# Group norm in token order with crossbar transposes of x, and a new order of the work

## The reference, cut to what matters

```python
def _gn(v, G=32, eps=1e-5):
    g = v.reshape(B_, H_, W_, G, C_ // G)
    m = jnp.mean(g, axis=(1, 2, 4), keepdims=True)
    s = jnp.var(g, axis=(1, 2, 4), keepdims=True)
    return ((g - m) / jnp.sqrt(s + eps)).reshape(v.shape)

qkv = x @ qkv_w.T + qkv_b            # q += x @ la_q.T @ lb_q.T, v += x @ la_v.T @ lb_v.T
attn = einsum('bqd,bkd->bqk', q * scale, k)      # 12 heads of 64, 196 x 196 per image and head
attn = attn + rel_h[..., None] + rel_w[..., None, :]   # q against tables of relative positions
out = softmax(attn) @ v
x + out @ proj_w.T + proj_b          # x was normalized by _gn before the attention only
```

## Time and profile before

| | |
|---|---|
| median of 3 runs | 3372.39 us (3372.22 to 3372.78) |
| the profiled execution | 3373.03 us, its span 3371.3 us |
| TensorE busy, share of the span | 3297.2 us, 98% |
| VectorE busy | 2528.2 us, 75% |
| ScalarE busy | 2098.2 us, 62% |
| SyncE's DMA queue, share of 16 engines | 49.8% |
| granted TensorE clock, mean | 0.991 |

### The profile page before, as it was taken

The page is one execution under the profiler, slowest core; times in us unless marked ns, Lnnn a source line. Parts: engine busy times, 40 slices in busy tenths (PEclk is TensorE's granted clock), DMA queues, the critical chain, the costliest instruction groups (busy, mean ns, idle before and its releaser), DMA issues.

```text
span 3371.3 us, 80148 instructions
## 1 busy us (share of the span) xinstructions
PE 3297.2 (98%) x31984; PEld 2130.7 (63%) x31984; DVE 2528.2 (75%) x5970; ACT 2098.2 (62%) x5651; POOL 35.8 (1%) x65
## 2 busy tenths in 40 slices
PE   7689999999999999999999999999999999999998
PEld 4456666666666666666666666666666666666665
DVE  7577777777777777777777777777777777777764
ACT  2466666666666666666666666666666666666664
POOL 0000000000000000000000000000000000000000
PEclk9799999999999999999999999999999999999999
DMA  3145664555555556565555555555565555565554
GB/s 128 42 96 109 120 122 103 115 113 112 118 121 107 113 112 114 116 121 107 110 116 113 112 123 118 101 117 111 110 127 120 100 118 108 111 126 122 103 106 105
DMA packets 1091412, 376.13 MB, mean 112 GB/s; under 512 B 916696, under 2 KB 1071320, under 8 KB 1091040
## 3 DMA queue, kind: packets, MB, share of 16 engines
q1 hardware_dynamic: 1075206, 333.63, 49.8%
q10 hardware_dynamic: 15834, 37.37, 3.9%
HBM read 86.60 MB, written 38.54 MB: 37 GB/s over the span
## 4 chain that ended last, share of the span: by engine, by line
PE 94%; DVE 2%; ACT 1%; issue 0%; DMA 0%; POOL 0%; SPq 0%; POOLq 0%; DVEq 0%
PE ring L556 51%; PE ring L623 17%; PE score L599 9%; PE o_ps L613 7%; PE ring L578 3%; PE ring L637 3%; PE ring L629 3%; ACT prob L682 1%; PE ring L642 0%; PE ring L563 0%; DVE split L789 0%; DVE row_max L769 0%; DVE rel_sb L762 0%; DVE split L781 0%; DVE rel_sb L756 0%
## 5 line engine op out<-in xcount | busy, mean ns | idle before, releaser
L556 PE MATMUL ring<-xn_hi,w_hi 128*128 128x392 f16 x3456 | 1143.2, 331 | 4.8 <-DVE xn_lo L839 4.6
L556 PE MATMUL ring<-xn_lo,w_hi 128*128 128x392 f16 x3456 | 1139.8, 330 | 0.0
L556 PE MATMUL ring<-xn_hi,w_lo 128*128 128x392 f16 x3456 | 1139.3, 330 | 0.5 <-issue 0.5
L682 ACT ACTIVATE prob<-score,neg_max,exp_scale 98x196 f32<-98x196 f32 x1536 | 769.8, 511 | 252.9 <-DVE neg_max L773 245.4
L769 DVE TENSOR_REDUCE row_max<-score 98x4 f32<-98x784 f32 x384 | 373.3, 972 | 273.2 <-PE score L599 272.1
L789 DVE SCALAR_TENSOR_TENSOR split<-prob,row_inv,split 98x196 f16<-98x196 f32 x1536 | 545.0, 417 | 7.8
L556 PEld LDWEIGHTS ring<-xn_hi,w_hi 128*128 128x128 f16 x3456 | 342.3, 99 | 260.7 <-issue 7.7
L556 PEld LDWEIGHTS ring<-xn_hi,w_lo 128*128 128x128 f16 x3456 | 338.8, 98 | 237.9 <-issue 3.6
L556 PEld LDWEIGHTS ring<-xn_lo,w_hi 128*128 128x128 f16 x3456 | 338.9, 98 | 208.3 <-issue 1.9
L623 PE MATMUL ring<-o_hi,w_hi 128*128 128x392 f16 x1152 | 380.2, 330 | 1.4 <-DVE o_lo L798 1.4
L623 PE MATMUL ring<-o_lo,w_hi 128*128 128x392 f16 x1152 | 379.8, 330 | 0.0
(11 more groups left out here) (118 smaller groups left out, 4896.7 us busy)
## 6 DMA issues: line engine op xcount, KB each, us to landing
y_sb<-in_x SPq DMA_DIRECT2D x192, 196.0 KB
out<-y_sb SPq DMA_DIRECT2D x192, 196.0 KB
x_sb<-in_x ACTq DMA_DIRECT2D x31, 1176.0 KB
rel_q<-rel_sb SPq DMA_DIRECT2D x128, 122.5 KB, 2.4
stage<-in_L_conv_qkv_w SPq DMA_DIRECT2D x3, 2304.0 KB, 15.4
turned<-split SPq DMA_TRANSPOSE x384, 4.2
rel_q<-rel_sb SPq DMA_DIRECT2D x128, 24.5 KB, 1.9
v_tok<-v_split SPq DMA_TRANSPOSE x192, 3.4
```

Of the source, the lines that this page charges most:

```text
L556: last = T.matmul(ring[:, bank, 0:NT], w[:, c, 128 * j:128 * j + 128], xx[:, par, c, :], start=(c == 0 and part == 0), stop=(c == CT - 1 a ...
L682: last = A.activation(prob[:, head, half, :], score[0:HALF, head, TOK * half:TOK * half + TOK], ACT.Exp, bias=neg_max[:, k % 2, i:i + 1], ...
```

## The change

The group norm is made on x as it is loaded, 98 tokens on partitions, instead of on transposed x, and the crossbar DMA does the turning afterwards, on fp16 parts.

- X and M are gone from TensorE, ScalarE and VectorE, and with them `xT`, `bn_stats` and `bn_aggr`.
- A (two a pair): VectorE sums x over the 24 channels of each group and two tiles, `tensor_reduce` of 98 x 1536. G0: a matmul with `gmean`, now 98 x 98 and filled with 1/(24 x 196), sums over tokens and spreads the means to all 98 partitions. B (two): subtract the mean, in place in `x_sb`. U (two): ScalarE squares into `squares`, which lies in the memory of `xs`. D (two): VectorE sums the squares. G1: variances of the 64 groups on partitions; `pow` on GpSimd; E makes a diagonal matrix; G2 spreads it by a matmul with ones. H (two): multiply, in place. I (two): ScalarE makes the fp16 high part in `xs`; L (two): VectorE the low part. XT (four): crossbar DMA of 112 x 1536 fp16 each, from `xs` to `xn`.
- Q, K and V read `xn[:, par, part, :, c, 0:98]`, four runs of 98 columns. Q0 waits once, for all four XT. The weights are no longer taken with a stride in `prepare`.
- LD waits until L of the pair before is done (`x_sb` is now in use until then) and stands in slot 5 instead of 6; A0 of the same pair stands at the end of VectorE's slot 6.
- `y_sb` has two buffers instead of three, `yT` one instead of two: ScalarE's Y now waits until Z of the block before is done.
- The five order lists are new. K and V stand a slot or so earlier in places, R1 has moved to slot 10 on VectorE and ScalarE. In SyncE's list CB, T0 and VT0 of a round stand ahead of the stores ST 4 and 5 and of the reloads.
- The memories that are zeroed have semaphores of their own, waited for at the first use.

The diff, cut to its core:

```diff
-YS = 3
+YS = 2
 PE_ORDER = (
+    each("S", 0, 0) + each("P", 1, 10) + each("Z", 2, 5) + each("V", 0, 0) + each("K", 0, 1)
+    + each("S", 0, 1) + each("P", 1, 11) + each("G", -1, 1) + each("V", 0, 1) + each("G", -1, 2) + each("Y", 1, 0)
+    + each("S", 0, 2) + each("P", 0, 0) + each("K", 0, 2) + each("Y", 1, 1) + each("Z", 1, 0)
+    + each("S", 0, 3) + each("P", 0, 1) + each("Y", 1, 2) + each("Z", 1, 1) + each("V", 0, 2)
+    + each("S", 0, 4) + each("P", 0, 2) + each("Z", 1, 2) + each("K", 0, 3) + each("Q", -1, 0)
...
+    + each("S", 0, 8) + each("P", 0, 6) + each("G", -2, 0) + each("Q", -1, 4, 5)
+    + each("S", 0, 9) + each("P", 0, 7) + each("K", 0, 5) + each("R", -1, 0) + each("Y", 1, 3) + each("R", -1, 1)
     + each("S", 0, 10) + each("P", 0, 8) + each("R", -1, 2, 3, 4) + each("V", 0, 5) + each("Y", 1, 4) + each("Z", 1, 3)
+    + each("S", 0, 11) + each("P", 0, 9) + each("K", -1, 0) + each("Y", 1, 5) + each("Z", 1, 4))
 ACT_ORDER = (
+    each("Y", 2, 5) + each("U", -1, 1) + soft(0) + each("V", 0, 0)
...
+    + each("Y", 1, 0) + each("I", -1, 0) + each("N", 0, 2) + each("K", 0, 2) + each("T", 0, 2) + each("I", -1, 1)
...
+    + each("Q", -1, 0) + each("P", 0, 3) + soft(5) + each("V", 0, 3) + each("LD", -2, 0)
...
+    + each("R", -1, 1, 2) + each("N", 0, 10) + each("R", -1, 3, 4) + each("T", 0, 10) + each("V", 0, 5)
+    + each("Y", 1, 4) + each("U", -2, 0) + each("P", 0, 9) + each("N", 0, 11) + each("K", -1, 0) + each("T", 0, 11))
 DVE_ORDER = (
+    each("S", 0, 0) + each("D", -1, 1) + soft(0) + each("Z", 2, 4) + each("V", 0, 0) + each("Z", 2, 5)
+    + each("S", 0, 1) + each("G", -1, 1) + each("K", 0, 1) + each("P", 1, 11) + each("E", -1, 0) + soft(1)
+    + each("G", -1, 2) + each("V", 0, 1) + each("H", -1, 0)
+    + each("S", 0, 2) + each("H", -1, 1) + each("N", 0, 2) + each("K", 0, 2) + each("T", 0, 2) + each("L", -1, 0)
+    + each("S", 0, 3) + each("Z", 1, 0) + each("P", 0, 1) + each("L", -1, 1) + soft(3)
...
+    + each("S", 0, 6) + each("Q", -1, 1) + each("N", 0, 6) + each("K", 0, 4) + each("T", 0, 6) + each("A", -2, 0)
+    + each("S", 0, 7) + each("Q", -1, 2) + each("P", 0, 5) + soft(7) + each("V", 0, 4) + each("A", -2, 1)
+    + each("S", 0, 8) + each("Q", -1, 3) + each("G", -2, 0) + soft(8) + each("Q", -1, 4) + each("B", -2, 0)
+    + each("S", 0, 9) + each("Q", -1, 5) + each("P", 0, 7) + each("N", 0, 9) + each("K", 0, 5) + each("T", 0, 9)
+    + each("R", -1, 0)
+    + each("S", 0, 10) + each("R", -1, 1, 2) + each("N", 0, 10) + each("R", -1, 3, 4) + each("T", 0, 10) + each("V", 0, 5)
     + each("S", 0, 11) + each("Z", 1, 3) + each("P", 0, 9) + each("N", 0, 11) + each("K", -1, 0) + each("T", 0, 11)
+    + each("B", -2, 1) + each("D", -2, 0))
 SP_ORDER = (
+    each("CB", 0, 0) + each("T", 0, 0) + each("VT", 0, 0)
+    + each("ST", 2, 4, 5) + each("T", 0, 1) + each("VT", 0, 1)
+    + each("LY", 1, 0) + each("XT", -1, 0) + each("LY", 1, 1) + each("T", 0, 2)
+    + each("XT", -1, 1, 2) + each("ST", 1, 0) + each("XT", -1, 3) + each("T", 0, 3) + each("LY", 1, 2)
+    + each("VT", 0, 2) + each("ST", 1, 1) + each("T", 0, 4) + each("LY", 1, 3)
+    + each("ST", 1, 2) + each("T", 0, 5) + each("VT", 0, 3) + each("LY", 1, 4)
...
+    + each("VT", 0, 5) + each("ST", 1, 3) + each("T", 0, 11) + each("LY", 1, 5))
...
+                elif kind == "XT":
+                    part, image = k // 2, k % 2
+                    wait(sp, xs_lo_made if part else xs_hi_made, 2 * p + image + 1)
+                    sp.sem_inc(sp_go, 1)
+                    sp.dma_start_transpose(xn[:, p % 2, part, 2 * image:2 * image + 2].rearrange("p b c r -> p (b c) r"),
+                                           xs[0:ROWS, part, 2 * image:2 * image + 2].rearrange("r b c -> r (b c)")
+                                           ).then_inc(xn_in, 16)
...
-                        if kind == "Q" and k == 0 and c % 2 == 0:
-                            wait(pe, xn_lo_made, 3 * p + c // 2 + 1)
+                        if kind == "Q" and k == 0 and c == 0:
+                            wait(pe, xn_in, 64 * p + 64)
...
+                    wait(act, done["Z"], 6 * p + k)
...
+                elif kind == "A":
+                    if k == 0:
+                        wait(dve, x_in, 16 * p + 16)
+                    two = slice(2 * k, 2 * k + 2)
+                    V.tensor_reduce(sums[:, k, :], x_sb[:, two, :].rearrange("p b (g c) -> p g b c", c=GP),
+                                    AX.XY, ALU.add).then_inc(summed, 1)
...
+                elif kind in ("B", "H"):
+                    wait(dve, read["G"], 3 * p + (1 if kind == "B" else 3))
+                    by_group = x_sb[:, 2 * k:2 * k + 2, :].rearrange("p b (g c) -> p b g c", c=GP)
+                    of = (mean if kind == "B" else rstd)[:, k:k + 1, :]
+                    V.tensor_tensor(by_group, by_group, of.unsqueeze(3).broadcast_to([HALF, 2, GROUPS, GP]),
+                                    ALU.subtract if kind == "B" else ALU.mult
+                                    ).then_inc(centred if kind == "B" else normed, 1)
```

More of the change, by code:

```diff
@@ L577, in _ @@
                                             "p (g i w) -> p g i w", i=n_rows, w=W)[:, :, i, :]
-                                    last = T.matmul(cols, tab[rows, ax, row, 32 * head:32 * head + 32], mov,
+                                    last = T.matmul(cols, tab[rows, ax, row, :], mov,
                                                     start=(part == 0), stop=(part == 2))
@@ L687, in _ @@
                     wait(act, row_inv_made, 12 * p + k + 1)
+                    if p == 0 and k == 0:
+                        act.wait_ge(split_zeroed, 1)
                     wait(act, pv_done, 12 * p + k - 1)
@@ new lines, in _ @@
+                elif kind == "A":
+                    if k == 0:
+                        wait(dve, x_in, 16 * p + 16)
+                    two = slice(2 * k, 2 * k + 2)
+                    V.tensor_reduce(sums[:, k, :], x_sb[:, two, :].rearrange("p b (g c) -> p g b c", c=GP),
+                                    AX.XY, ALU.add).then_inc(summed, 1)
+                elif kind == "D":
+                    wait(dve, squared, 2 * p + k + 1)
+                    two = slice(2 * k, 2 * k + 2)
+                    V.tensor_reduce(sums[:, k, :], squares[:, two].rearrange("p b (g c) -> p g b c", c=GP),
+                                    AX.XY, ALU.add).then_inc(summed, 1)
+                elif kind == "G" and k == 1:
+                    wait(dve, done["G"], 3 * p + 2)
+                    V.tensor_scalar(var_eps[:, :], ring[0:2 * GROUPS, bank, 0:1], EPS, None,
+                                    ALU.add).then_inc(read["G"], 1)
+                elif kind == "E":
+                    wait(dve, inv_dev_made, p + 1)
+                    V.tensor_scalar(diagonal[:, :], ident[0:2 * GROUPS, 0:2 * GROUPS], inv_dev[:, :], None,
+                                    ALU.mult).then_inc(diagonal_made, 1)
+                elif kind == "G":
+                    wait(dve, done["G"], 3 * p + k + 1)
+                    to = mean if k == 0 else rstd
+                    V.tensor_copy(to[:, :, :].rearrange("p n g -> p (n g)"),
+                                  ring[0:HALF, bank, 0:2 * GROUPS]).then_inc(read["G"], 1)
+                elif kind in ("B", "H"):
[5 more added lines that the diff above has]
+                                    ).then_inc(centred if kind == "B" else normed, 1)
```

236 lines of the change are left out of this document (88 added, 148 removed).

## The result

The kernel after takes 3322.8 us (median of 4 runs, 3321.4 to 3323.5) against 3372.3 for the kernel before: 0.985 of its time, with a 95% interval of 0.9838 to 0.9863. The profiled execution took 3322.35 us, with a span of 3320.5. The forecast was 3303 in a range of 3282 to 3350.

The account below looks back on a forecast made before the run. TensorE's own work, busy 100 of 100 us, was taken as the bound. 3373.0 - 97.0 (removed) + 9.3 (G) + 6 (waits) + 10 (start) + 2 (end) = 3303.3, against the median 3303; range 3282 to 3350.

Parts of the forecast that it names:

- The likeliest case: Steady state: TensorE stays the bound and waits under 0.7 us a pair; 3282 to 3322 us, chance 0.60.
- Removed, -97.0: TensorE: the 24 transposes of x a pair, 3.18 us, vanish over 30.5 pairs; -97.0 us.
- G, +0.3 a pair: TensorE: three G matmuls a pair instead of two, two of them wider; +9.3 us over 31 pairs (3 to 28).
- Waits, +0.2 a pair: TensorE kept waiting by VectorE, which enters slot 0 late; 0.2 us a pair, +6 us in all (0 to 31).
- S1 (slack 1.5): Scores block of slot 1 on TensorE: VectorE's lateness from slots 10 and 11 leaves it 1.5 us of slack.
- the ring: Banks behind Z4 and Z5, read by VectorE at the end of slot 0: 0.6 us of slack.
- The moved stores: nothing: SyncE's queue: moving stores 4 and 5 behind T0 and VT0 gains nothing, as no steady-state P waits for a transfer.
- Start, +10: Before the steady state: the longer norm chain to Q0 costs 8 us, pair 1's x load 2; +10 (7 to 16).
- End, +2: Last round: reload 5 waits for store 3, 2.2 us; +2 us (0 to 5).
- (a): Slots 10 to 1: VectorE late by more than its slack, TensorE waits about 1.2 us a pair; 3334 us, chance 0.27.
- (b): Crossbar transfers of x keep Q0 waiting 2 us, plus 1.3 at the 1.2 GHz level; 3405 us, chance 0.11.
- (c): The DMA engines become the bound, at nine times T's cost per byte for XT; about 3,950 us, chance 0.02.

## Why the prediction was right, and where its sizes were off

The likeliest case came true in its mechanism: TensorE's own work shrank, and it waits under 0.7 us a pair (0.56 of idle over 500 to 3000 us). The time is 0.8 us above that case's own edge of 3322, and inside the stated range. Of the signs, XT's landing, the large operations and the G blocks (0.64 a pair) were as named; the period (98.17 for 97.6), TensorE's 100 of 100 and the 24 us to Q0 were not. By stretches the miss of 19.8 us is almost whole: 10.2 in the middle (-71.5 where -97.0 + 9.3 + 6 = -81.7 stood), 5.9 at the start, 2.9 at the end.

- *Removed, -97.0.* Right for the order of time on TensorE: 3.18 a pair are gone from the balance, and the cover that I named for the four runs of `xn` held. That as much comes back is another matter: in the kernel before, three quarters of it gave 47 us for 73. I reckoned TensorE at 100 of 100 as bound by its own work alone. VectorE was a step behind it in several places, without a row to show it. What the new order of the lists gave by itself is open: but for the stores, no run has it alone.
- *G, +0.3 a pair.* The blocks themselves cost 0.21 more, by rows.
- *Waits, +0.2 a pair.* Mis-sized: 0.40 ahead of G2 and about 0.07 ahead of G0 (P's gain), and they are the largest part of the middle's miss; some 0.16 a pair more are spread over Q, K, V, S and R. The step that failed is the list of what VectorE owes in slots 0 and 1. It had S1 (slack 1.5) and the ring (0.6), not E and P11, on which G2 and Y0 wait; with 1.75 us added, all 1.75 came through. I took VectorE to be 2.5 us late there with 1.5 to spare; it is late with nothing to spare.
- *The moved stores: nothing.* Against the kernel before the term may stand, but its reason was wrong. I read from the earlier trace rows of before that no P waits for a transfer. With Z4 behind D1 and soft 0 in VectorE's list, the old order costs 46.9 us, as VT0 then lands late for P0. Had the change been made without this part, it would have ended at 0.999 of the time before. That case was in none of my rivals.
- *Start, +10.* It was +15.9. The chain had no term for a first `pow`: in the kernel before the last memset ends at 94.98 and `pow` comes at 101.92, 0.16 behind the end of `var_eps`, so that a pause of 6.8 just fits in unseen. Moved out of the chain, it gave 6.1. Pair 1's G0, for which I had put 2 with the load, gave 5.1 in the run with G0 later.
- *End, +2.* It was +4.9. In the last round, where Q0 to Q5 are missing, slot 8 has no block of Q, K or V between its S and the next, and S9 waits for the exps; before, V4 stood there. The waits ahead of S6 to S9 are 8.2 us together, where the kernel before has 4.5 ahead of S6 and S8, and with one `yT` two of the last Z blocks wait 0.92 us each instead of 0.42. This is read from the traces alone; no run tries it. The wait of S9, the longest, in order of time on TensorE:

```profile
3259.99 0.40 PE L597 MATMUL score<-k_hi,q_hi 64*98 64x196 f16 x2 [4.51 <-ACT prob L686]
```

- *Rivals.* (a) was right in its mechanism and is what the middle's miss consists of, at a third of its price. (b) did not happen: XT lands in 3.8 us, as T does in 4.2. Its price was somewhat low: it put 1.3 us on top of a wait of 2, and a wait of 3.0 measured 5.0 to 5.1, 2.0 on top. (c) is refuted by the DMA share of 0.65, and with it the price of the Trainium skill, "VectorE: DVE Perf Modes", section "The three transpose paths", of 1309 ns a block, for transfers of many blocks: XT's twelve land together in 3.8 us.

## What to carry to other kernels

When the bound engine is busy for 100 of 100, ask of each block to be removed which other engine's work it covers, slot by slot: here such cover took back 0.8 of 2.4 us a pair in the kernel before. When a step moves back in an engine's list, go through every queue that waits for it, and judge the queue's order in the kernel as it will be; an order of SyncE's queue that cost nothing before cost 47 us after. And a library operation's first use belongs where nobody waits.

## What the runs showed of the hardware

- The first `pow` on GpSimd stands behind 6.8 us in which nothing runs, in the loop and in the preparation alike (6.8 to 7.5 in the runs of the kernel after and its variants); the later ones start 0.22 us behind `var_eps`'s start (1542.94, 1543.16).
- After 2.9 us of idle, TensorE ran at its 1.2 GHz level for some ten matmuls of 392 columns, 0.33 us from one to the next, before it was back at 0.166.
- A wait of 0.38 us inside TensorE's stream costs 0.54, as the next matmul finds the pipeline empty.
- A load of 1.2 MB beside four crossbar transfers, at the start, made TensorE wait 7 us longer for them (18.9 instead of 11.8).
